# Convolution, attention and expert network on one core: the middle of the kernel in quarters of four images instead of halves of eight

## What is computed

```
x  = group_norm(h, 32);  x = silu(conv1x1(x, w0, b0))
x  = group_norm(x, 16);  x = silu(conv3x3(x, w1, b1, groups=4))    # 64 -> 128 channels
x  = group_norm(x, 2)                                              # "gn3"
a  = mean over 8x8 windows of x;  a = max over the two radix halves
a  = silu(conv1x1(a, w2, b2));  a = group_norm(a, 8)               # "gna"
a  = conv1x1(a, w3, b3);  gate = softmax(a over the two radix halves)
out = weight^T (x * gate, summed over radix)
h  = h + group_norm(out, 32)                                       # "gn4", gives x1
# tokens: T = 16 images (time), N = 256 pixels, D = 64 channels
n  = layer_norm(x1);  e = score . tanh(fc n)
x1 = x1 + causal softmax-weighted mean of n over images s <= t     # a scan over the images
n  = layer_norm(x1)                                                # "ln2"
w  = softmax(mean over images of n @ Wr)                           # 8 experts, per pixel
x1 = x1 + sum_e w_e * (relu(relu(n W1_e) W2_e) Wo_e + bo_e)
```

## Time and profile before

| | us |
|---|---|
| median of 3 runs | 155.56 |
| the runs | 154.56 to 156.14 |
| the profiled execution, as timed | 154.75 |
| its span, first to last instruction | 152.8 |

### The profile page before, as it was taken

One profiled execution on the slowest core, in us unless ns is written; L12 is line 12 of the kernel. 1 busy time (PEld: TensorE's weight loads), 2 busy tenths in 40 slices (PEclk: granted clock), 3 DMA queues, 4 the chain that ended last, 5 costly groups with the idle time before them and its releaser, 6 DMA issues.

```text
span 152.8 us, 2584 instructions
## 1 busy us (share of the span) xinstructions
PE 129.6 (85%) x951; PEld 58.6 (38%) x953; DVE 102.1 (67%) x305; ACT 78.0 (51%) x162; POOL 31.0 (20%) x28
## 2 busy tenths in 40 slices
PE   6977999999034698699597999999999999999991
PEld 2332343443032145258372461575524442223220
DVE  0586875842757644606989698549886519999951
ACT  3002360945991445563031698745488997642630
POOL 8032702004044020800444208000250000000000
PEclk9999999999965559999968999999999999999999
DMA  4993000000000000000000000000000000000304
GB/s 113 408 369 93 0 6 0 4 0 0 2 0 0 4 0 0 0 0 0 2 4 0 0 0 0 0 4 0 0 0 4 0 0 6 0 0 0 111 26 137
DMA packets 3835, 4.95 MB, mean 32 GB/s; under 512 B 240, under 2 KB 3440, under 8 KB 3696
## 3 DMA queue, kind: packets, MB, share of 16 engines
q1 hardware_dynamic: 3680, 4.60, 9.0%
q10 hardware_dynamic: 144, 0.20, 0.6%
HBM read 3.75 MB, written 1.05 MB: 31 GB/s over the span
## 4 chain that ended last, share of the span: by engine, by line
PE 60%; DVE 24%; ACT 6%; POOL 5%; issue 4%; POOLq 0%
PE bank L1043 10%; PE bank L883 8%; PE bank L1016 8%; PE bank L1029 7%; DVE ctxs L713 4%; PE bank L831 3%; PE bank L933 2%; PE bank L895 2%; PE bank L900 2%; DVE y L651 2%; PE bank L925 2%; PE bank L838 2%; PE bank L814 2%; ACT y L380 1%; DVE s_wst L596 1%
## 5 line engine op out<-in xcount | busy, mean ns | idle before, releaser
L439 ACT ACTIVATE h<-bank,s_bnb 128x512 f32<-128x512 f32 x22 | 14.5, 691 | 10.0 <-PE bank L1016 10.0
L883 PE MATMUL bank<-pad,w 32*64 32x512 f32 x288 | 17.7, 595 | 0.2 <-DVE pad L554 0.2
L1016 PE MATMUL bank<-xs,f1s 64*64 64x512 f32 x128 | 17.1, 605 | 0.3 <-issue 0.2
L1029 PE MATMUL bank<-h,f2s 64*64 64x512 f32 x128 | 17.1, 603 | 0.3 <-ACT more L447 0.2
L831 PE MATMUL bank<-warm 128*128 128x512 bf16 x32 | 9.8, 464 | 1.3 <-POOL warm L323 1.3
L883 PEld LDWEIGHTS bank<-pad,w 32*64 32x64 f32 x288 | 6.8, 130 | 8.7 <-issue 7.8
L349 ACT ACTIVATE act<-bank,par 128x512 f32<-128x512 f32 x4 | 2.8, 689 | 13.1 <-PE bank L844 13.0
L738 DVE TENSOR_SCALAR h<-bank,s_bnb 128x512 f32<-128x512 f32 x10 | 7.5, 749 | 2.8 <-PE bank L1016 2.8
L955 PE MATMUL bank<-ctxs,par 128*128 128x128 f32 x32 | 6.6, 334 | 2.3 <-DVE ctxs L713 2.3
L838 PE MATMUL bank<-warm 128*128 128x512 bf16 x26 | 8.0, 440 | 0.3 <-issue 0.2
L895 PE MATMUL bank<-y,par 128*64 128x512 f32 x16 | 6.3, 928 | 2.0 <-DVE y L651 2.0
(11 more groups left out here) (246 smaller groups left out, 256.3 us busy)
## 6 DMA issues: line engine op xcount, KB each, us to landing
par<-params SPq DMA_DIRECT2D x1, 1516.0 KB, 9.4
xin<-x SPq DMA_DIRECT2D x4, 256.0 KB, 4.2
out<-act SPq DMA_DIRECT2D x4, 256.0 KB, 2.2
row_par<-row_params SPq DMA_DIRECT2D x4, 160.0 KB, 8.8
w<-conv_w SPq DMA_DIRECT2D x1, 288.0 KB, 5.3
par<-params ACTq DMA_DIRECT2D x1, 193.5 KB, 3.8
```

Source lines behind the costliest of these rows:

```text
L439: A.activation(h1[(2 * m + h) % 4][:], bank[Z1[h]][:], ACT.Relu, bias=tile("bnb", P, 3 * EP)[:, col:col + 1]).then_inc(h1_ready, 1)
L883: ins = T.matmul(bank[CONV1[k][2 * j + h]][at:at + C, :], w1[rows, tap, :], pad[rows, b:b + 2, dy:dy + S, dx:dx + S], start=(tap == 0), st ...
L1016: ins = T.matmul(bank[Z1[h]][to, :], f1s[own, e, to], xs[own, k, q], start=True, stop=True)
L1029: ins = T.matmul(bank[Z2[h]][at:at + C, :], f2s[rows, h, e, :], h1[(2 * m + h) % 4][rows, :], start=True, stop=True)
```

## The change

After the 3x3 convolution the batch goes on in quarters k = 0 to 3 (`NQ` = 4, `BQ` = 4 images, `PQ` = 2 pairs). A quarter's two pixel halves lie side by side in one bank, so the steps from `ln1` to `xt` are one for each quarter. Quarter k is the units 2k and 2k + 1 of the convolution, and all of it has one order of channels (k % 2), so that `w2` and `w3` are one product each in place of two. All quarters use the one small bank. `gn3` takes the window's max before the norm, so that `win` has two DVE instructions and `gn3` has four. `xr` adds up over the quarters, `logits` is two products in place of four. An expert unit is (k, e, h). The mixes go quarter by quarter, the output is stored by quarters with whole rows of 256 pixels. The number of `heat` steps falls from 14 to 2. `ORDER` is new throughout. Cut to its core:

```diff
+NQ = 4
+STRIPS = NQ
+PQ = PAIRS // NQ
+BQ = B // NQ
...
-    s2row.0 conv.12 gn3.0 conv.13 conv.14 gn3f.0 silu.6 win.0 conv.15 conv.16 conv.17 ws.4 w2.0 ws.5 silu.7 ws.6 gna.0 gnaf.0 ws.7 gn3.1
-    wan.0 gn3f.1 gate.0 ynorm.1 gate.1 w3.0 win.1 outp.0 gn4.0 gn4f.0 heat.0 heat.1 ynorm.2 x1.0 heat.2 w2.1 heat.3 ln1.0 heat.4 tok.0
-    heat.5 heat.6 gna.1 heat.7 heat.8 ln1.1 ynorm.3 hn.0 heat.9 hn.1 hch.0 hch.1 fc.0 fc.1 coef.0 score.0 att.0 cen.0 heat.10 heat.11
-    heat.12 gnaf.1 scan.0 wan.1 cen.1 ln2.0 w3.1 heat.13 gate.2 gate.3 ln2.1 outp.1 xn2.0 xt.0 gn4.1 xn2.1 l1.0 gn4f.1 d1.0 xt.1 x1.1 t2.0
...
+    gn2f.1 conv.4 conv.5 conv.6 norm0.1 ws.0 conv.7 conv.8 ws.1 s2row.0 ws.2 conv.9 conv.10 gn3.0 conv.11 conv.12 silu.3 gn3f.0 conv.13
+    ws.3 win.0 w2.0 ynorm.0 conv.14 gna.0 gn3.1 gnaf.0 conv.15 conv.16 w3.0 conv.17 gn3f.1 silu.4 wan.0 silu.5 win.1 gate.0 w2.1 silu.6
+    outp.0 ws.4 gna.1 ws.5 ynorm.1 gnaf.1 gn3.2 gn4.0 silu.7 gn3f.2 w3.1 gn4f.0 wan.1 win.2 x1.0 w2.2 gate.1 tok.0 gna.2 ws.6 outp.1
+    gnaf.2 ws.7 ln1.0 ynorm.2 heat.0 gn4.1 wan.2 w3.2 gn4f.1 gn3.3 hn.0 heat.1 x1.1 hch.0 gn3f.3 gate.2 tok.1 win.3 ln1.1 fc.0 w2.3 outp.2
+    gna.3 score.0 gn4.2 gnaf.3 hn.1 ynorm.3 coef.0 cen.0 w3.3 wan.3 gn4f.2 att.0 scan.0 x1.2 hch.1 gate.3 ln2.0 tok.2 ln1.2 fc.1 s1row.0
+    outp.3 cen.1 gn4.3 xn2.0 gn4f.3 hn.2 t2.0 xt.0 x1.3 score.1 hch.2 coef.1 l1.0 tok.3 d1.0 fc.2 att.1 scan.1 d1.1 ln1.3 xr.0 l1.1 l2.0
+    ln2.1 score.2 l1.2 coef.2 l2.1 cen.2 hn.3 hch.3 d1.2 att.2 xn2.1 l2.2 l1.3 scan.2 fc.3 xt.1 d1.3 xr.1 ln2.2 score.3 coef.3 l1.4 l2.3
+    cen.3 d1.4 att.3 scan.3 l1.5 l2.4 d1.5 xn2.2 ln2.3 d1.6 l1.6 l2.5 xn2.3 xt.2 l1.7 l2.6 xt.3 d1.7 xr.2 l1.8 l2.7 l1.9 d1.8 xr.3 d1.9
+    logits.0 l2.8 l1.10 t2.1 wt.0 l2.9 wb.0 wb.1 l1.11 l2.10 t2.2 t2.3 l1.12 l2.11 mix.0 mix.1 l1.13 l2.12 mix.2 mix.3 l1.14 l2.13 mix.4
+    mix.5 l1.15 l2.14 mix.6 mix.7 mix.8 mix.9 l2.15 mix.10 mix.11 mix.12 mix.13 mix.14 mix.15 mix.16 mix.17 mix.18 mix.19 mix.20 mix.21
+    mix.22 mix.23 finish.0 mix.24 mix.25 finish.1 mix.26 mix.27 mix.28 mix.29 mix.30 finish.2 mix.31 finish.3
...
-        CHAIN = ((5, 6), (0, 1))
+        CHAIN = (5, 1, 7, 0)
+        CONTEXT = (6, 1, 7, 0)
...
-        units = [(k, q, e, h) for k in range(NK) for q in range(Q) for e in range(EP) for h in range(2)]
+        units = [(k, e, h) for k in range(NQ) for e in range(EP) for h in range(2)]
...
             def gn3_stats(k):
 
-                dve.wait_ge(y_squared, BK * (k + 1))
-                V.tensor_reduce(tile(f"wsum{k}", P, 2, BK)[:, 0, :], tile(f"wst{k}", P, BK, WIN), AX_X, ALU.add).then_inc(stats_ready, 1)
+                dve.wait_ge(y_squared, BQ * (k + 1))
+                sums = tile(f"wst{k}", P, BQ, WIN)
+                V.tensor_reduce(tile(f"wsum{k}", P, 2, BQ)[:, 0, :], sums, AX_X, ALU.add).then_inc(stats_ready, 1)
+                other = tile(f"wino{k}", P, BQ, WIN)
+                V.tensor_copy(other[0:32], sums[32:64])
+                step(V.tensor_copy(other[64:96], sums[96:128]))
+                step(V.tensor_tensor(tile(f"wmax{k}", P, BQ, WIN), sums, other, ALU.max))
...
             def small(name):
 
-                _, _, free, at = small_of(name)
-                if at > 1:
-                    pe.wait_ge(free, at - 1)
-                elif name in SMALL2_AT:
-                    pe.wait_ge(y_ready, BK // 2 + 1)
+                if SMALL_AT[name] > 1:
+                    pe.wait_ge(small_free, SMALL_AT[name] - 1)
...
             def out_product(k):
+                pe.wait_ge(gated_y_ready, k + 1)
...
+                j = k % 2
+                for h in range(2):
+                    s = k * BQ + 2 * h
+                    ins = T.matmul(bank[CHAIN[k]][h * C:(h + 1) * C, :], w("weight")[:, j * C:(j + 1) * C], y[:, s:s + 2, :], start=True, stop=True)
+                ins.then_inc(outconv_done, 1)
...
+            def fc(k):
+                pe.wait_ge(hch_ready, k + 1)
+                T.matmul(bank[CHAIN[k]][:], w("fc"), hch[:, k, :], start=True, stop=True).then_inc(fc_done, 1)
...
             def weights_spread():
                 small(("wb", 0))
-                pe.wait_ge(ctx_added, Q * NK)
+                pe.wait_ge(ctx_added, 2)
```

More of the change, by code:

```diff
@@ L77 @@
[L77 to L80, removed]
+    warm.0 warm.1 warm.2 warm.3 silu0.0 silu0.1 warm.4 warm.5 gn1.0 warm.6 warm.7 spr.0 warm.8 gn1f.0 warm.9 warm.10 silu.0 gn1.1 xnorm.0
@@ L240, in positions @@
             return {s: i + 1 for i, s in enumerate(found)}
[L243 to L251, removed]
+        SMALL_AT = positions({"gn1", "gn2", "s1row", "s2row", "gn3", "w2", "gna", "w3", "gn4", "score", "logits", "wt", "wb"}, {("wb", 1)})
         given = positions({"gn1", "gn2", "gn3", "win", "gna", "wan", "gn4"})
@@ L257, in conv_attention_experts @@
         for name, k in ORDER:
-            parts = {"gn1f": [("gn1", P, PK)], "gn2f": [("gn2", P, PK)], "gn3f": [("gn3", P, BK)], "gnaf": [("gna", C, BK)],
-                     "gn4f": [("gn4", P, PK)], "bn": [("bnv", P, 3 * EP)],
-                     "ln1": [("ln1", P, BK)], "ln2": [("ln2", P, BK)]}.get(name, [])
+            parts = {"gn1f": [("gn1", P, PK)], "gn2f": [("gn2", P, PK)], "gn3f": [("gn3", P, BQ)], "gnaf": [("gna", C, BQ)],
+                     "gn4f": [("gn4", P, PQ)], "bn": [("bnv", P, 3 * EP)],
+                     "ln1": [("ln1", P, Q * BQ)], "ln2": [("ln2", P, Q * BQ)]}.get(name, [])
             for part, rows, cols in parts:
@@ L288, in context_at @@
         def context_at(k, q, t):
-            return 2 * (k * BK + t - 1) + q + 1
-        mixes = sorted(range(NU), key=lambda n: (units[n][1], units[n][0], n))
+            return 2 * (k * BQ + t - 1) + q + 1
         PER_OUT = 2 * EP
@@ L305, in _ @@
                 sp.dma_start(row_par[s * STRIP:(s + 1) * STRIP], row_params).then_inc(rows_loaded, 16)
[L307 to L313, removed]
+            for k in range(NQ):
+                sp.wait_ge(res_ready, k + 1)
+                sp.dma_start(out_pairs[pairs_of(k)].rearrange("b p n -> p b n"), res[:, pairs_of(k), :]).then_inc(out_stored, 16)
+            sp.wait_ge(out_stored, 16 * NQ)
         @block.gpsimd
@@ L784, in _ @@
                 "s1row": lambda k: scale_first_layer(), "s2row": lambda k: scale_second_layer(),
-                "ws": window_stats, "gn3": gn3_stats, "gn3f": lambda k: group_finish(("gn3", k), BK), "win": window_in,
-                "w2": window_half, "gna": window_norm_stats, "gnaf": lambda k: group_finish(("gna", k), BK, C),
-                "wan": window_normalise, "gate": gate_y, "gn4": gn4_stats, "gn4f": lambda k: moments_finish(("gn4", k), PK),
+                "ws": window_stats, "gn3": gn3_stats, "gn3f": lambda k: group_finish(("gn3", k), BQ), "win": window_in,
+                "w2": window_half, "gna": window_norm_stats, "gnaf": lambda k: group_finish(("gna", k), BQ, C),
+                "wan": window_normalise, "gate": gate_y, "gn4": gn4_stats, "gn4f": lambda k: moments_finish(("gn4", k), PQ),
                 "x1": residual1, "ln1": lambda n: layer_norm_stats("ln1", n), "hn": lambda k: layer_norm_scale("ln1", k, hn_ready),
```

427 lines of the change are left out of this document (197 added, 230 removed).

## The result

| | before | after |
|---|---|---|
| median, us | 155.7 (4 runs) | 146.74 (4 runs, 146.66 to 146.95) |
| span of the profiled execution, us | 152.8 | 144.9 |
| that execution as timed, us | 154.75 | 146.95 |

The ratio is 0.945, with a 95% interval of 0.941 to 0.948. The changed kernel is 9.0 us faster by the medians and 7.9 us by the spans. Now and then an execution takes over 1.5% longer than the fastest of the same kernel; the medians and ranges of this document leave such executions out.

A forecast was written before the change was run, and what follows sets the result against it. DVE was taken to bound the kernel up to `l1.0` and PE behind it: 83.5 + 60.8 + 2.6 = 146.9 us for `finish.3`, 3.25 behind it, span 150.2, 2.6 less than before; median 153.0 us, range 149.5 to 158.5.

The forecast's parts named there:

- The gate of quarter 0: Behind the convolution: gating of y for quarter 0 starts at 39.5 us against 46.96, 7.4 us earlier.
- DVE from `gate.0` to `d1.0`: DVE stretch ahead of `l1.0`: 41.2 us of work plus 4.7 of waits from 39.25, so `d1.0` at 85.2 us.
- 98 small ones at 0.19 (18.6): Small DVE instructions between `gate.0` and `d1.0`, each charged 0.19 us, 18.6 us of the 41.2.
- PE behind `l1.0`: PE from `l1.0` to `finish.3`: 60.8 us of work where it was 62.8, plus 2.6 of stalls.
- The stalls: PE's waits behind `l1.0`, left at 2.6 us as before, bounds 0.5 and 6.
- The three chains from `score` to `xt`: Behind `l1.0`, `score` to `xt` comes three times instead of once, with `l1` and `l2` duos of earlier quarters ready each time.
- The clock: PE ahead of `l1.0`: half clock from 44 to 64 us, full from there on.
- each microsecond at half there delays `l1.0` by nearly 0.5 us: Price of half clock before `l1.0`, from 16 us of PE work at full clock in the last 17.5 us.
- the tail: Behind `finish.3`: one DVE pass and one store, 3.25 us, taken as unchanged.
- rivals with 3 to 8 us in them: Slower side: clock stays down before `l1.0`, 158 us, chance 0.17; DVE at 85% or 80%, 155.6 or 158.6, chance 0.25.
- the lower only one: Higher gain: if the clock holds, PE's chain parts up to 64 us take half the time; 150 us, chance 0.13.
- DVE doesn't reach 90%: DVE ahead of `l1.0`: at 85% busy the gain is gone, 155.6 us; at 80%, 158.6; chance 0.25.

The follow-up runs named there:

- heat_back: The changed kernel with 15 heat steps instead of 2, the new ones in PE's waits from `gna.1` on; 145.36 us, ratio 0.936 to the kernel before.
- shift_first: The changed kernel with `x1` cut in two, its small DVE instruction that ACT waits for one step earlier in the order; 146.05 us.

## Why the prediction was wrong in size

**The gate of quarter 0.** Forecast 39.5 us, measured 38.73; the convolution ends at 39.2 against 39.6. Right but for 0.8 us.

**DVE from `gate.0` to `d1.0`.** Forecast 39.25 + 41.2 + 4.7 = 85.2; measured 38.47 (the gate's scalar) to 81.36, 42.9 us, of which 4.9 are waits and 38.0 work. The sum of the waits and the engine were right, with waits of 2.8 us at `x1` (2.4 forecast), 1.4 for PE (2.3) and 0.6 for ACT elsewhere (none). The term that failed is "98 small ones at 0.19 (18.6)": counted from start to start, less the named waits, they took 16.1 us, 0.165 each. That is 2.5 us; the large passes were 21.9 against 22.6. With the 0.8 at the gate, and less 0.2 for the waits, this makes the 3.8 us by which `d1.0` came early. DVE in the changed kernel shows why:

```profile
44.38 0.17 DVE L519 SCALAR_TENSOR_TENSOR s_gn4v0raw<-s_gn4v0raw 128x4 f32<-128x4 f32 x1
44.46 0.16 DVE L493 COPY s_gn3v2ms<-bank 128x8 f32<-128x8 f32 x1
44.66 0.16 DVE L495 SCALAR_TENSOR_TENSOR s_gn3v2sq<-s_gn3v2ms 128x4 f32<-128x4 f32 x1
44.85 0.16 DVE L496 SCALAR_TENSOR_TENSOR s_gn3v<-s_gn3v2ms,s_gn3v2sq 128x4 f32<-128x4 f32 x1
45.10 0.16 DVE L528 TENSOR_REDUCE s_gn4v0ms<-bank 128x2 f32<-128x4 f32 x1
45.18 0.15 DVE L529 TENSOR_REDUCE s_gn4v0ms<-bank 128x2 f32<-128x8 f32 x1
```

An instruction that waits for DVE's own last result starts 0.20 us behind it (44.46 to 44.66, 44.66 to 44.85). One that doesn't, starts 0.08 us behind it (44.38 to 44.46, 45.10 to 45.18), while the first is still under way. I charged all at the waited price. The cut also lets an unlike step stand between two that depend on each other, so more of them are of the cheap kind: 23 of 98 start less than 0.095 us behind the one before, where it was 10 of 55 in the kernel before. There the small ones took 0.175 us each, so a part of the miss could be read beforehand. DVE's busy time rose by 9.1 us (102.1 to 111.2), where I had 14.1. The Trainium skill, "VectorE: DVE Perf Modes", section "The TRN2 errata", which the prediction weighed, has the formula that gives, as an estimate, 165 ns for 8 columns; the rows have 150 to 170 ns, so it fits the duration. The same page's section "The DRAIN you can't avoid" says that leaving out the semaphore between chained copies saved nothing, and that a next instruction that isn't held starts earlier. On instructions this small the rows agree with the second, 0.08 against 0.20 us.

**PE behind `l1.0`.** Work: 60.8 us forecast, 61.8 measured; the difference to before, 2.0 forecast, 2.2 measured. Right. The stalls, left at 2.6 us, were 0.3 (1.4 before, by PE's busy time; the 2.6 had taken 1.2 us of work for stalls). The three chains from `score` to `xt` found enough `l1` and `l2` duos to lie under, as the prediction said and then didn't price. Together 62.1 us and not 63.4.

**The clock.** I had half clock from 44 to 64 us and priced each further microsecond at 0.5. It lasted to 72 with a gap of 3, and holding it up for most of the stretch was worth 1.4 us in all (heat_back). The step that failed is "each microsecond at half there delays `l1.0` by nearly 0.5 us": it took PE's work as the only path, where DVE's ran close beside it. shift_first shows how close it was to being right: take some of DVE's waits away, and the clock decides.

**The range.** The spans: 150.2 forecast, 144.9 measured; of these 5.3 us, 3.9 are `l1.0`'s start, 1.3 the stretch behind it and 0.1 the tail. The remaining 1.0 us of the miss is the step from one execution to a median: I added 2.8 us to the span (1.95 around it and 0.8 for an execution below the median), and the changed kernel has 1.8. The upper side of the range had rivals with 3 to 8 us in them, the lower only one, and that one hung on the clock. No rival said that a price of the sum could be too high, though 98 instructions carried it.

**"DVE doesn't reach 90%".** It was busy for 35.4 of 42.9 us, 83%, and still had little time to give: of 4.05 us of further instructions, 2.7 came out at `l1.0`. Busy time leaves out the few hundredths of a microsecond between two instructions; the sum of the waits named in the trace (4.9 us, 11%) is the better measure.

## What to carry to other kernels

When a chain of short steps through four engines has waits everywhere, cutting the batch finer pays only if the order lets the pieces overlap: the same quarters cost 14 us in lockstep and gave 9 us when interleaved. Whether the interleaving alone, without the finer cut, would do as well, no run here says. Find the engine that will be full afterwards, price its small instructions by their distances from start to start, waited and unwaited apart, and check the bound by adding a few useless ones at one place in both kernels. A lower PE clock costs only what some engine waits for: twelve `heat` steps were worth 3.0 us in the kernel before, thirteen 1.4 us in the changed one and 1.7 us with the shift. And before you explain a few tenths of a microsecond between two traces, look whether they are there ahead of the first edited step.

## What the runs showed that I had not expected

- Small DVE instructions of 2 to 16 columns: most are 0.15 to 0.18 us long whatever their columns (a reciprocal 0.20, one that reads the bank 0.23), 0.20 us from start to start when each waits for the one before, 0.08 us when it doesn't.
- The reciprocal root on POOL takes 0.70 us on 2 columns, 1.00 on 4 and 1.64 on 8, which bears out the 0.7 that was taken for `gn4`:

```profile
46.07 0.70 POOL L328 TENSOR_TENSOR s_gn4v0r<-s_gn4v,minus_half 128x2 f32<-128x2 f32 x1
```

- Two `heat` steps less cost 1.3 us in the changed kernel by the medians, although the mean clock of the profiled execution rose: its half clock lay under `fc.1`, for which DVE's `s1row` waits.
